# A second gate that scatters its rows into expert stretches, in one block with the experts stage behind it

## What is computed

```python
def _L1_ffn_ref(x, W1, b1, Wg, bg, Wd, bd):        # x: layer-normed rows
    H = gelu(xf @ W1 + b1)                         # 8192 x 512, shared by all experts
    probs = softmax((H @ Wg + bg) / TEMP, axis=-1) # 8 experts
    assign = argmax(probs, axis=-1)
    for e in range(8):
        y = H @ Wd[e] + bd[e]
        out = out + where(assign == e, probs[:, e:e+1] * y, 0)
...
x = x + _L1_ffn_ref(_layernorm(x), ...)
```

## Times and profile before

| | us |
|---|---|
| median of 3 runs | 1575.52 (1574.82 to 1575.8) |
| the profiled execution | 1568.44 |
| its span, first to last instruction | 1566.7 |
| `gate1`, `route`, `experts_out` begin (first operation) | 1201.5, 1330.6, 1364.4 |

### The profile page before, as it was taken

How to read it: one execution, slowest core, us unless ns; L and a number is a source line. 1 busy time by engine, 2 the same in 40 slices (tenths; PEclk the granted TensorE clock), 3 DMA queues, 4 the chain that set the end, 5 groups by cost and what they waited for, 6 DMA issues and landing times. The chain is left out here.

```text
span 1566.7 us, 28942 instructions
## 1 busy us (share of the span) xinstructions
PE 1191.2 (76%) x6576; PEld 864.8 (55%) x6577; DVE 868.6 (55%) x3882; ACT 826.3 (53%) x2276; POOL 570.5 (36%) x871
## 2 busy tenths in 40 slices
PE   2444413558746999999959999999996997587776
PEld 1223303547635999999935554455443453476665
DVE  5777899956586334355567743444445675611111
ACT  3555535415546666666627765665554664543332
POOL 3666425500001777477667200000000000167775
PEclk9999955768768999999969999999998999799998
DMA  9400000001100333333311000000000321322221
GB/s 260 108 1 1 1 1 1 1 1 55 55 0 9 80 85 89 67 84 85 86 49 48 19 1 0 0 0 0 1 0 0 81 80 54 14 70 74 78 71 45
DMA packets 86042, 68.81 MB, mean 44 GB/s; under 512 B 18678, under 2 KB 74815, under 8 KB 85964
## 3 DMA queue, kind: packets, MB, share of 16 engines
q1 hardware_dynamic: 71500, 36.45, 8.8%
q0 software_dynamic: 14464, 31.52, 8.0%
HBM read 41.68 MB, written 26.77 MB: 44 GB/s over the span
## 5 line engine op out<-in xcount | busy, mean ns | idle before, releaser
L1696 POOL DMA_INDIRECT g_Z<-z,sitter x72 | 70.6, 980 | 510.3 <-SPq L1682 482.4
L1594 ACT ACTIVATE c_H<-ps,c_b 128x128 f32<-128x128 f32 x576 | 156.9, 383 | 97.6 <-PE ps L1642 97.5
L1461 POOL DMA_INDIRECT c_Z<-z,sitter x108 | 103.2, 955 | 250.0 <-POOLq L1291 202.5
L2077 PE MATMUL ps<-BIG,w_ihT 128*128 x364 | 156.2, 578 | 3.3 <-ACTq L2090 3.3
L1642 PE MATMUL ps<-c_ZT,c_w 128*128 128x128 f32 x1152 | 143.3, 278 | 2.7 <-ACT c_ZT L1583 2.7
L1628 PE MATMUL ps<-w_dn,c_H 128*128 x1152 | 140.7, 275 | 0.6 <-ACT c_H L1594 0.6
L1642 PEld LDWEIGHTS ps<-c_ZT,c_w 128*128 128x128 f32 x1152 | 137.0, 195 | 3.3 <-ACT c_ZT L1583 3.3
L1628 PEld LDWEIGHTS ps<-w_dn,c_H 128*128 128x128 f32 x1152 | 134.7, 192 | 0.9 <-issue 0.9
L1748 ACT ACTIVATE g_H<-ps,bias_cols 128x256 f32<-128x256 f32 x144 | 60.4, 471 | 112.5 <-PE ps L1785 111.8
L2077 PEld LDWEIGHTS ps<-BIG,w_ihT 128*128 128x128 f32 x364 | 69.6, 192 | 84.8 <-issue 84.8
L2085 PE MATMUL ps<-e_hs,w_hhT 128*128 128x512 f32 (+1 forms) x256 | 110.0, 572 | 0.0
(11 more groups left out here) (515 smaller groups left out, 2765.5 us busy)
## 6 DMA issues: line engine op xcount, KB each, us to landing
y<-c_ys SPq DMA_DIRECT2D x72, 128.0 KB
z<-ZB SPq DMA_DIRECT2D x32, 256.0 KB, 2.9
z<-X SPq DMA_DIRECT2D x16, 256.0 KB, 3.9
w_up<-in_L_ffn_W_dram SPq DMA_DIRECT2D x1, 2048.0 KB
w_dn<-in_L_ffn_W_dram SPq DMA_DIRECT2D x8, 256.0 KB
w_dn<-in_L_ffn_Wd_dram SPq DMA_DIRECT2D x8, 256.0 KB
c_Z<-z,sitter POOLq DMA_INDIRECT x108, 2.5
g_Z<-z,sitter POOLq DMA_INDIRECT x72, 2.8
```

The lines of the kernel that those rows point to most:

```text
L1461: pool.indirect_dma_start(Z[t % 2][h][:, :], None, z, bass.IndirectOffsetOnAxis(ap=k.sitter[:, t * HALVES + h:t * HALVES + h + 1], axis=0) ...
L1594: act.activation(H[u][:, c, h * P:(h + 1) * P], UP[u][c // 2][:, o:o + P], ACT.Gelu, bias=b1[u][h][:, c:c + 1]).then_inc(gelu, 1)
L1696: pool.indirect_dma_start(Z[t % DEPTH][h][:, :], None, z, bass.IndirectOffsetOnAxis(ap=k.sitter[:, t * HALVES + h:t * HALVES + h + 1], axis=0)
L2077: last = pe.matmul(view(k.ps[4 * u + j], wide, lanes), k.w_ihT[:, w, :], state(i, u, s, p, wide, lanes), start=True, stop=(s == 0))
```

## The change

- `route` is gone for the last block; so are the store of weights, the one-hot matrices, `k.sitter` and `k.place`.
- `z` gets one stretch for each expert (8192 + 256 rows each) and one block of padding. A row is 258 words: 128 normalized, 128 of `X`, the weight, and the token's number.
- DVE writes the rows into a ring of 6 pairs of groups in SBUF (`k.R`), which lies over expert and LSTM weights that nothing reads any more. `back` writes the sum to the ring instead of `X`; it waits for the ring's old scatters.
- Inside the gate's loop, for each pair of groups: `pick` and `seat` (DVE) choose the expert and compute the seat as stretch + rank, `rank` (PE, 11 bfloat16 matmuls) makes the rank from running sums, `tanh_of` (ACT) stands in for Exp. DVE interleaves `pick` with `spread`, and `seat` with `root_of` (the two halves of the old `scale`).
- POOL then scatters the pair's 8 tiles into `z`, one indirect DMA for each. SP's stores of group rows are gone.
- The gate's loop is written out (no loop instructions), and runs `lift` and `back` five groups ahead (`LIFTED = 5`): three of them all in step 0.
- After the loop, counts give padding positions (8 stores by SP) and tables of base row and expert for each block.
- The experts stage is in the same block. SP fetches each 128-row block with an ordinary DMA at a base row that it loads into a register, eight tiles ahead (`DEPTH = 8`), into dead `BIG`; results wait in dead `X`. POOL only places, by the token numbers in the row. Before the first fetch SP waits for the tables, all paddings and all scatters.

```diff
-ROW = 2 * D + 1
+ROW = 2 * D + 2
+STRIDE = B * N + 2 * P
+RING = 6
+LIFTED = 5
-DEPTH, BEHIND = 4, 4
+DEPTH = 8
...
+    PICKED = [2 * q + 3 for q in range(PAIRS - 2)] + [GROUPS - 2]
+    def ahead(g):
+        return range(3, LIFTED + 1) if g == 0 else range(g + LIFTED, min(g + LIFTED + 1, GROUPS))
...
+    def gate_sync(sp):
+        sp.wait_ge(s_sel, 1)
+        sp.dma_start(z[E * STRIDE:E * STRIDE + P, :], pad[:, :]).then_inc(padded, 16)
+        sp.wait_ge(s_pad, 1)
+        for e in range(E):
+            free = sp.value_load(pad_at[0:1, e:e + 1], min_val=0, max_val=E * STRIDE - P)
+            sp.dma_start(z[ds(free, P), :], pad[:, :]).then_inc(padded, 16)
+    def gate_gpsimd(pool):
+        for q in range(PAIRS):
+            pool.wait_ge(weighted, q + 1)
+            pool.wait_ge(seated, q + 1)
+            for n in range(q * PAIR, (q + 1) * PAIR):
+                pool.indirect_dma_start(z, bass.IndirectOffsetOnAxis(ap=k.seats[:, 0, n:n + 1], axis=0),
+                                        k.R[:, row(n), :], None, bounds_check=E * STRIDE - 1, oob_is_err=False
+                                        ).then_inc(scattered[q % RING], 16)
...
+        for g in range(GROUPS + 1):
+            if g > 0:
+                dve.wait_ge(scores, g)
...
+                dve.tensor_copy(sc[:, :], SC[:, :]).then_inc(scores_sb, 1)
+            if g < GROUPS - 1:
+                normalized(g + 1)
...
+            elif g % 2 and g + 3 < GROUPS:
+                spread((g + 3) // 2, beside)
+            elif g % 2 == 0 and g + 2 < GROUPS:
+                root_of((g + 2) // 2, beside)
...
+            if 0 < g < GROUPS - LIFTED:
+                back(g + LIFTED)
...
+        finish(pick(PAIRS - 1))
+        dve.sem_inc(counted, 1)
+        finish(seat(PAIRS - 1))
...
+        def tanh_of(q):
+            act.wait_ge(shifted, q + 1)
+            if q >= 1:
+                act.wait_ge(weighted, q)
+            act.activation(tanh[:, :, :], k.LG[:, tiles_of(q), :], ACT.Tanh, scale=0.5).then_inc(tanhed, 1)
...
+            for n in ahead(g):
+                turn_back(n)
+            for c in range(C):
+                act.wait_ge(up, g * C + (c + 1))
...
+                act.activation(H[u][:, c, :], UP[c][:, :], ACT.Gelu, bias=k.b_up1[:, c:c + 1]).then_inc(gelu, 1)
+                if c == 1:
+                    for q in range(PAIRS - 1):
+                        if PICKED[q] + (q == PAIRS - 2) == g:
+                            tanh_of(q)
...
+        def rank(q, biased):
...
+            pe.matmul(RANK, k.ones16[:, :], apart[:, None, :].to_broadcast([P, PAIR, E]), start=True, stop=False)
+            pe.matmul(RANK, k.ones16[:, :], sums[:, q:q + 1, :].to_broadcast([P, PAIR, E]), start=False, stop=False)
+            for n in range(PAIR):
+                pe.matmul(RANK[:, n * E:PAIR * E], k.ones16[:, :], marks[:, 0:(PAIR - n) * E], start=False, stop=False)
+            pe.matmul(RANK, k.upper16[:, :], marks, start=False, stop=True).then_inc(ranked, 1)
...
+    Z = [[k.BIG[:, n * ROW:(n + 1) * ROW] for n in range(b * HALVES, (b + 1) * HALVES)] for b in range(DEPTH)]
+    ys = [[k.X[:, n, :] for n in range(b * HALVES, (b + 1) * HALVES)] for b in range(DEPTH)]
+    def experts_sync(sp):
+        sp.wait_ge(k.tabled, 1)
+        sp.wait_ge(k.padded, 16 * (E + 1))
+        for b in range(RING):
+            sp.wait_ge(k.scattered[b], 16 * PAIR * len(range(b, GROUPS // 2, RING)))
+        def fetch(t, b, r):
+            if not (isinstance(t, int) and t < DEPTH):
+                sp.wait_ge(placed[b], r * (16 * HALVES))
+            for h in range(HALVES):
+                at = sp.value_load(k.base[0:1, ds(t * HALVES + h, 1)], min_val=0, max_val=E * STRIDE)
+                sp.dma_start(Z[b][h][:, :], z[ds(at, P), :]).then_inc(fetched[b], 16)
+        rounds(sp, fetch, NT, DEPTH + 4, 0)
+    def experts_gpsimd(pool):
+        for t in range(NT):
+            b = t % DEPTH
+            pool.wait_ge(y_ready, t + 1)
+            for h in range(HALVES):
+                pool.indirect_dma_start(out, bass.IndirectOffsetOnAxis(ap=Z[b][h][:, ROW - 1:ROW].bitcast(I32), axis=0),
+                                        ys[b][h][:, :], None, bounds_check=B * N - 1, oob_is_err=False
+                                        ).then_inc(placed[b], 16)
...
-        gate1(nc, k, sem, z1)
-        route(nc, k, sem, "t", k.K1, SLOTS1, z1)
-        experts_out(nc, k, sem, z1, out.rearrange("b n d -> (b n) d"))
+        gate1_experts_out(nc, k, sem, z1, out.rearrange("b n d -> (b n) d"))
```

More of the change, by code:

```diff
@@ new lines, in gate1_parts @@
+    best, first, total, pos = (mine(n, [P, PAIR]) for n in ("best", "first", "total", "pos"))
+    tied, tanh, prod = (mine(n, [P, PAIR, E]) for n in ("tied", "tanh", "prod"))
+    token = mine("token", [P, TILES], I32)
+    K16, sums, apart = mine("K16", [P, TILES, E], BF16), mine("sums", [P, PAIRS + 1, E], BF16), mine("apart", [P, E], BF16)
+    part, pad, stride = mine("part", [P, E]), mine("padding", [P, ROW]), mine("stride", [1, E])
+    cnt, nb, end, gap = (mine(n, [1, E]) for n in ("cnt", "nb", "end", "gap"))
@@ new lines, in experts_scalar, with turn_out, step @@
+    def experts_scalar(act):
+        def turn_out(t, u):
+            act.wait_ge(turned, t + 1)
+            act.activation(ZT[u][:, :], TR[u][:, 0:SLOT_TILE], ACT.Copy).then_inc(turned_sb, 1)
+        def step(t, b, r):
+            u = b % 2
+            if isinstance(t, int) and t == 0:
+                turn_out(0, 0)
+            if not (isinstance(t, int) and t < 2):
+                act.wait_ge(dn, t - 1)
+            for c in range(C):
+                if c % 2 == 0:
+                    act.wait_ge(up, t * C + (c + 2))
+                act.activation(H[u][:, c, :], UP[u][c // 2][:, c % 2 * SLOT_TILE:(c % 2 + 1) * SLOT_TILE],
+                               ACT.Gelu, bias=k.b_up1[:, c:c + 1]).then_inc(gelu, 1)
+            if not (isinstance(t, int) and t == NT - 1):
+                turn_out(t + 1, 1 - u)
+        rounds(act, step, NT, 2, 2)
@@ L1711, in _ @@
[L1711 to L1712 removed]
+            gate[1](pool)
+            experts[1](pool)
         @block.vector
         def _(dve):
[L1716 to L1730 removed]
@@ L1731, in _ @@
[L1731 removed]
+            gate[2](dve)
+            experts[2](dve)
         @block.scalar
         def _(act):
[L1735 to L1751 removed]
@@ L1752, in _ @@
-            rounds(act, step, NT, 2, 2)
+            gate[3](act)
+            experts[3](act)
         @block.tensor
         def _(pe):
-            w2 = k.w_dn1[:, :, :, :].rearrange("p e c d -> p (e c d)")
-            def turn(t, b, r):
-                pe.wait_ge(fetched[b], (r + 1) * (16 * HALVES))
-                if not (isinstance(t, int) and t < 2):
-                    pe.wait_ge(turned_sb, t - 1)
-                for h in range(HALVES):
-                    last = pe.transpose(TR[b % 2][:, h * P:(h + 1) * P], Z[b][h][:, 0:D], k.ident[:, :])
-                last.then_inc(turned, 1)
@@ L1793, in _ @@
-            rounds(pe, step, NT, 2, 2)
+            gate[4](pe)
+            experts[4](pe)
 def gnn1(nc, k, sem, y):
```

694 lines of the change are left out of this document (334 added, 360 removed).

## The result

The changed kernel takes 1512.53 us (median of 4 runs, 1510.94 to 1516.51) where the kernel before took 1575.62: a ratio of 0.9604 (95% interval 0.9586 to 0.9623), 63 us less. The forecast was 1514.5 us, in a range of 1502 to 1540. The profiled execution took 1510.94 us with a span of 1509.2 (before 1568.44 and 1566.7), 57.5 us less.

What follows compares the result with a forecast made beforehand. PE bounds the gate's loop, a chain the hand-over, and POOL's four indirect DMAs for a tile the experts stage. Terms 9.4 (gate) - 20.9 (hand-over) - 49.5 (experts) = -61 us gave a median of 1514.5 us, range 1502 to 1540.

Steps and rivals of the forecast that it cites:

- POOL's four DMAs for a tile: Experts stage: 1.30 us each held a tile to 5.20 us; with two, PE's 3.73 sets the pace, -49.5 us.
- The ranks: Gate loop: seven ranks of 11 narrow matmuls, 0.102 us each, add 7.9 us; bounds 0 and twice that.
- The fifteen steps: Gate loop, first to last scores: short steps throughout, 93.05 us for 98.7, plus the ranks: +2.2 us.
- 9 us later: Sign of being right, at the gate's end: the last logits come 9 us later than before.
- The hand-over: Last logits to the experts' first transpose: POOL's scatter backlog ends it, 23.7 us in place of 44.6, -20.9.
- The start: Start of the gate: three lifts in step 0 ahead of the first Gelu, +5.2, and 2 for PE's clock: +7 us.
- The tail: Last place to the end of the span: 6.2 us, with no change forecast.
- the 149 by which the prediction was to stand or fall: Experts stage to the span's end: 148.8 us where it was 198.2; if not near 149, the prediction falls.
- SP's fetch pace: Rival, experts stage: register load and issue take 2.6 us, so tiles stay at 5.20; 1567 us, chance 0.06.
- DVE's limit: Rival, gate loop: DVE's small operations make each pair 1.5 us longer, +10 us, 1524.5; chance 0.12.
- The slower case: Rival, gate: scatters beside busy DVE take 1.7 us or more, POOL falls behind; 1595 at 2.8 us; slower chance 0.05.
- The table loads: Rival, gate loop: each Tanh between Gelus costs two loads of 1.28 us, 7 us in all, 1521.5; chance 0.23.

Runs made afterwards that it cites:

- run with four DMAs: Changed kernel with two further indirect gathers on POOL for each tile of the experts stage, into memory nobody reads: 1562.92 us, ratio 0.9961 to the kernel before.
- run with four buffers: Changed kernel with four buffers for the experts' fetched tiles in place of eight: 1636.29 us, ratio 1.0424 to the kernel before.
- run with more backlog: Changed kernel with eight idle indirect gathers on POOL ahead of the last pair's scatters: 1520.20 us, ratio 0.9686 to the kernel before.
- runs with early Gelus: Changed kernel with step 0's Gelus ahead of two copies and PE's lift 5 later, alone or with DVE's group 4 addition earlier: 1511.60 and 1510.61 us.
- run with two blocks: Changed kernel with its one block cut in two again, gate and experts: 1513.52 us, ratio 0.9644 to the kernel before.
- one with one DRAIN more: Changed kernel with one further DRAIN on POOL between the gate's last scatter and the first place: 1508.11 us, ratio 0.9588 to the kernel before.
- run above: Changed kernel with the weights from Exp in place of Tanh, three small DVE operations fewer for a pair: 1527.30 us, ratio 0.9714 to the kernel before.

## Why the prediction was right

The mechanism that carried most of the sum, POOL's four DMAs for a tile, held, and its term came to 0.2 us (-49.3 for -49.5), with up projections 3.73 us apart as forecast. The run with four DMAs shows the cause and the run with four buffers the condition, which the prediction did not price: it asked only whether POOL, SP, ACT and DVE fit under PE's 3.73 us, not how many buffers a loop through place, landing and fetch needs. Of the smaller terms four were mis-sized:

*The ranks.* "11 x 0.102 x 7 = 7.9 us" took a weight load in the open for the cost of each narrow matmul; in a train a rank costs 0.30 us, so 7 x 0.30 = 2.1. That is 5.8 us less. The fifteen steps came out only 4.4 us under the forecast (-2.2 for +2.2): of the other 1.4, 0.85 is the first scores, which ran at the lower clock, and most of the rest is the last step, 6.93 us for some 6.2, in which PE waits 0.82 us for DVE's seats. So the last logits came 3.4 us later than before and not 9.4: the sign "9 us later" failed.

*The hand-over*, 26.0 us in place of 23.7. POOL's backlog ended it, as put and as the run with more backlog shows. Pair 5's first scatter came 11 us ahead of the last logits' end, not 12.6, because the two ranks between them are short: 1.6 us of the gain there is lost here. The other 0.8 is SP's register load ahead of its first fetch (1350.43, when its wait for the scatters ends, to 1351.24), which the sum left out. The second fetch is issued 1.13 us behind the first, for 0.4 in the sum, but its rows are there 2.2 us after that, for 2.9; these two cancel.

*The start*, +5.5 in place of +7. The first up projection began 1.9 us earlier (12.1 for 14.0 from the first operation), where 1.5 was forecast, and the slower clock cost less than the 2 us taken ahead of the first scores; the 0.85 within them is counted in the steps. The chain to the fourth Gelu came out as put: it ends at 1228.43, 5.1 us later than the scores began before, for 5.2. But PE comes later still, which the sum did not have: its last lift waits 3.49 us for DVE, and with the transposes behind it PE reaches the scores at 1228.85. The runs with early Gelus move ACT's order and this lift together, so they don't tell the two apart; they do show that both are worth only 2 us at the end.

*The tail.* "6.2 from there to the end of the span" was carried over unchanged, and was 11.9. The step took the end for fixed, but POOL's DRAIN grew. That one block now holds both stages' DMAs is 3.3 of the 5.7 us, as the run with two blocks and the one with one DRAIN more show; the other 2.4 stay open. So the experts stage to the end of the span took 154.6 us, and not the 149 by which the prediction was to stand or fall; to the last place's end it took 143.7, for 143.5.

The sum of the terms was -61 and the stage gave -58.9; the stages before gave back 1.4. That the sum came so near is in part luck: the gate was put 6 us too dear, and hand-over and tail together 8 us too cheap. The profiled execution was forecast at 1507.4 and took 1510.9. The median came out nearer, because the 7.1 us by which before's profiled run lay below its median were carried over, while after's lay only 1.6 below: two errors that partly cancel.

Of the rivals, SP's fetch pace fell (it issues a tile's two fetches in 2.24 us, from 1351.24 to 1353.48, and later it and POOL wait in nearly every tile), and so did DVE's limit (PE has hardly a gap in the loop). The slower case fell too: scatters at 984 ns beside a DVE busy 73 of 94 us, far from the 1.7 us at which POOL would fall behind. The Trainium skill ("SBUF — State Buffer", warning on "The DVE blocks DMA trap (SWDGE)") says that DVE in a 2-port mode locks POOL out of writing descriptors; no scatter of this case shows such a lock for certain: the median is 0.984 us, and why one of 64 took 1.33 is open. The table loads fell as well: eight Tanhs at 0.256 us without a load, between Gelus. The Trainium skill ("ScalarE: Activation LUTs", section "Table sets: the hidden batching unit") lists tanh apart from gelu's set; the trace differs from that here, and agrees with it for Exp, whose loads the run above shows. By the Trainium skill's price ("ScalarE: Activation LUTs", section "What ACT_TABLE_LOAD costs") of 2.66 us for a switch that run would have had some 5.3 us for each pair, an estimate; there the two loads took 2.57 us and the pair 2.3 more.

## What to carry to other kernels

Count what an engine issues for each tile before buying depth, and then count the depth: a fetch moved to another queue is tied to the release of its buffer, and an order that puts the next tiles' input ahead of this tile's output spends buffers (here two of them). When stages are merged into one block, look at what the block's end has to wait for, and put that work where the engine idles. Where the stages ahead of the change scatter by more than the effect, measure from the change's first operation.

## What was not expected of the hardware

*POOL's DRAIN behind indirect DMAs.* It takes 1.35 us behind 16 places and 5.93 behind 72, and ends 5.28 us behind the last of 64 scatters or gathers: 0.082 to 0.085 us for each indirect DMA since the DRAIN before. But the measures differ (the first two are lengths, behind a wait for the places to land; the third is a distance from the last DMA's end), and not all DRAINs fit. The three among the places end 3.0, 2.2 and 2.1 us behind the last of 24, 16 and 16, about 0.13 for each. Longer stretches take less for each: 9.19 us behind 136, and the same with eight gathers more; 4.94 behind the 208 of the run with four DMAs for a tile; one in an earlier stage ends 8.57 us behind the last of 208; 3.64 behind the 144 mixed gathers and places of the kernel before, 4.95 with eight buffers there. So the count alone does not give the length. What is shown is that a further DRAIN shortens the one behind it; what sets the length is open.

*Narrow matmuls overlap.* Eleven bfloat16 matmuls, each with a weight load of its own (ten of them of the same weights), start 0.02 to 0.04 us apart (1249.75, 1249.79, 1249.82, and the eleventh at 1250.03), though a lone weight load shows 0.102 us.

*Tanh and Gelu run from one table here, Exp and Gelu don't*: no load against two of 1.28 us for a pair.
